# A graph network with attention and experts on one core: layer 2's joint products ahead of its spreads, the gate's arithmetic behind layer 1's last task, attention rows normalised on ScalarE, layer ends reordered

## What is computed

```python
for W, a_s, a_d, bg, R, g, b in layers:      # widths 3 -> 64 -> 128 -> 64
    h = _gat(x, src, dst, W, a_s, a_d, bg)   # softmax over a joint's edges, weighted sum of x @ W
    x = gelu(layer_norm(h + x @ R, g, b))
pose = layer_norm(x.reshape(n, J * 64) @ fpW + fpb, fng, fnb)
h = concatenate([pose, txt], axis=1)
h = h + attn(layernorm(h))     # silu, short convolution, normalised queries through a two-layer memory
h = h + ffn(layernorm(h))      # 8 experts of width 512, top two by router, gelu
```

## Time and profile before

| | us |
|---|---|
| median of 3 runs | 4580.26 (4574.3 to 4583.47) |
| the profiled execution | 4576.98 |
| its span, first to last instruction | 4575.1 |
| PE busy | 3889.9 (85%) |
| DVE busy | 3668.4 (80%) |
| ACT busy | 2318.4 (51%) |
| POOL busy | 1527.8 (33%) |

### The profile page before, as it was taken

The page is one execution under the profiler, slowest core; times in us unless marked ns, Lnnn a source line. Parts: engine busy times, 40 slices in busy tenths (PEclk is TensorE's granted clock), DMA queues, the critical chain, the costliest instruction groups (busy, mean ns, idle before and its releaser), DMA issues.

```text
span 4575.1 us, 62001 instructions
## 1 busy us (share of the span) xinstructions
PE 3889.9 (85%) x22762; PEld 1797.7 (39%) x22762; DVE 3668.4 (80%) x6623; ACT 2318.4 (51%) x3705; POOL 1527.8 (33%) x1513
## 2 busy tenths in 40 slices
PE   4878898888988888898888988888888888988888
PEld 2232343434334343343334434343343433434345
DVE  3878888788887888878788887888878888887872
ACT  2544455454545545455454555545455454554543
POOL 2524324252432524324252332524315243242410
PEclk8898999999999999999999999999999999999999
DMA  2000000000000000000000000000000000000000
GB/s 91 1 3 1 2 5 1 3 3 3 3 1 3 3 3 3 2 5 1 3 3 3 4 1 3 3 3 3 1 6 1 3 3 2 5 1 3 3 2 6
DMA packets 22815, 22.95 MB, mean 5 GB/s; under 512 B 3378, under 2 KB 21818, under 8 KB 22122
## 3 DMA queue, kind: packets, MB, share of 16 engines
q1 hardware_dynamic: 22506, 18.93, 1.4%
HBM read 14.72 MB, written 4.19 MB: 4 GB/s over the span
## 4 chain that ended last, share of the span: by engine, by line
DVE 48%; PE 34%; issue 9%; ACT 8%; POOL 1%; DVEq 0%; SPq 0%; DMA 0%; ACTq 0%; POOLq 0%
DVE R L2068 13%; PE bank L1033 6%; PE bank L1042 5%; DVE X L2073 4%; PE bank L764 3%; PE bank L836 3%; DVE X L1767 2%; PE bank L902 2%; DVE R L2043 2%; ACT X L1403 2%; DVE X L2105 2%; PE bank L776 2%; DVE Ho L2254 2%; DVE R L2046 1%; PE bank L680 1%
## 5 line engine op out<-in xcount | busy, mean ns | idle before, releaser
L576 POOL TENSOR_TENSOR X<-X,R 128x512 f32<-128x512 f32 (+1 forms) x624 | 801.0, 1284 | 1134.0 <-DVE X L2073 1131.3
L2068 DVE TENSOR_TENSOR R<-bank,R 128x1024 f32<-128x1024 f32 (+1 forms) x624 | 738.4, 1183 | 47.9 <-DVE X L2073 1.0
L2105 DVE TENSOR_TENSOR X<-X,bank 128x1024 f32<-128x1024 f32 (+2 forms) x432 | 484.7, 1139 | 248.4 <-PE bank L804 124.9
L1033 PE MATMUL bank<-XT,c_w 128*128 128x512 f32 x1024 | 565.6, 670 | 90.4 <-DVE R L2068 49.9
L1403 ACT ACTIVATE X<-X,c_vec 128x1024 f32<-128x1024 f32 (+2 forms) x432 | 498.1, 1173 | 217.8 <-DVE X L2105 214.4
L1042 PEld LDWEIGHTS bank<-c_w,SQ 128*128 128x128 f32 x4096 | 492.1, 192 | 95.8 <-issue 89.0
L1042 PE MATMUL bank<-c_w,SQ 128*128 128x128 f32 x4096 | 514.5, 278 | 0.0
L940 PE MATMUL bank<-X,WR 64*128 64x512 f32 (+1 forms) x832 | 482.1, 661 | 36.4 <-DVE Ho L2254 31.4
L1444 ACT ACTIVATE R<-bank 128x512 f32<-128x512 f32 (+1 forms) x416 | 241.2, 580 | 527.0 <-PE bank L902 296.6
L902 PE MATMUL bank<-R,c_W 64*128 64x512 f32 (+1 forms) x832 | 473.9, 651 | 37.6 <-ACT R L1446 24.1
L2073 DVE SCALAR_TENSOR_TENSOR X<-bank,bgc,R 128x512 f32<-128x512 f32 (+1 forms) x624 | 456.0, 731 | 31.7 <-PE bank L956 10.0
(11 more groups left out here) (287 smaller groups left out, 6675.9 us busy)
## 6 DMA issues: line engine op xcount, KB each, us to landing
c_w<-in_w SPq DMA_DIRECT2D x2, 2048.0 KB
out<-Ho SPq DMA_DIRECT2D x32, 128.0 KB, 1.9
c_fpW<-in_fpW SPq DMA_DIRECT2D x1, 3200.0 KB
X<-in_x SPq DMA_DIRECT2D x34, 75.0 KB, 2.0
X<-in_txt SPq DMA_DIRECT2D x32, 64.0 KB, 1.9
X<-in_sel SPq DMA_DIRECT2D x1, 600.0 KB
X<-in_sel SPq DMA_DIRECT2D x1, 300.0 KB
X<-in_raw SPq DMA_DIRECT2D x1, 256.0 KB
```

The costliest lines, as they stand in the source:

```text
L576: TT(dst, dst, TQ[:, k % 3, 0:cols], ALU.subtract).then_inc(zs_ok, 1)
L1033: mm(hidden_bank(e, m), w1[:, k * P:k * P + P], XT2[:], start=True, stop=True).then_inc(hid_ps, 1)
L2068: TT(TQ[:, k % 3:4:3 - k % 3, 0:cols], bR[k % 2][:, :, 0:cols], both, ALU.mult).then_inc(t_ok, 1)
L2105: TT(dst, dst, b, ALU.mult).then_inc(u_ok, 1)
```

## The change

- **Layer 2.** From n = 1 on PE issues `product_d` of the next task ahead of `spread_alpha`. DVE does `joint_differences` of the next task between its multiplication 2068 and its sum 2073, no longer after the sum.
- **The gate.** The six parts of `top_two` stand behind the last task of layer 1, ahead of `rstd`.
- **The attention's norm** moves from DVE (four instructions, subtract and multiply in one) to ACT (eight: four with the mean as bias and scale -1, four with the standard deviation's inverse as scale), after its copies of n = 1 and n = 2. The sign is taken back in `token_columns` (scale -1). In the window `add_expert` 7 now stands ahead of the moments.
- **Layer ends with experts.** `up` unit 0 writes bank 0 and waits for ACT's last copy (`d_sb`) instead of the last multiplication; that wait now stands ahead of unit 1. `HD` uses slots 2 to 5, and ACT does `hidden` unit 0 of experts 0 and 4 ahead of its last square, as soon as the last but one `variance` is done. Before the sums are turned, PE waits for that `hidden`.
- **POOL's `mean_differences`** waits for the third exp (`exp_ok`), no longer for the copied scores.

```diff
-        HD = SQ[:, 0:MT, :]
+        HD = SQ[:, 2:2 + MT, :]
+            if e in (0, 4):
+                return bank[(0, 2, 1, 2)[m]]
...
             def mean_differences(s, l):
-                pool.wait_ge(s_ok, s * 2 + l)
+                pool.wait_ge(exp_ok, s * 7 + 3 * l + 1)
...
@@ TensorE, graph_layer
+                    early = l == 2 and n > 0
+                    if early and n + 1 < NT[l]:
+                        product_d(s, l, n + 1)
                     spread_alpha(s, l, n)
-                    if n + 1 < NT[l]:
+                    if not early and n + 1 < NT[l]:
                         product_d(s, l, n + 1)
...
                 if tail:
-                    pe.wait_ge(t_ok, s * AGG + T0[l] - NT0 + NT[l] + 1)
+                    pe.wait_ge(d_sb, s * AGG + T0[l] - NT0 + NT[l])
                     up(s - 1, e, (0,))
                 variance(s, l, BATCHES[l] - 2)
                 if tail:
+                    pe.wait_ge(t_ok, s * AGG + T0[l] - NT0 + NT[l] + 1)
                     up(s - 1, e, (1,))
                 variance(s, l, BATCHES[l] - 1)
+                if tail:
+                    pe.wait_ge(hid_sb, (s - 1) * E * MT + e * MT + 2)
...
@@ ScalarE, graph_layer
+                    if l == 1 and n in (1, 2) and tail:
+                        attention_norm(s - 1, n - 1)
+                    if n == NT[l] + 2 and moe:
+                        hidden(s - 1, 0 if l == 1 else 4, (0,))
                     if n >= 3:
                         square(s, l, n - 3)
...
+            def attention_norm(t, part):
+                act.wait_ge(an_ok, t + 1)
+                if part == 1:
+                    act.wait_ge(hc_ok, t + 1)
+                for k in range(4):
+                    if part == 0:
+                        last = A_(Xn[:, k, :], HN[:, k, :], ACT.Identity, bias=mv[:, k, 0:1], scale=-1.0)
+                    else:
+                        last = A_(Xn[:, k, :], Xn[:, k, :], ACT.Copy, scale=rs[:, k:k + 1])
+                last.then_inc(ho_ok if part else hc_ok, 1)
...
@@ hidden on ScalarE
+                if units == (0,) and e in (0, 4):
+                    act.wait_ge(v_ps, (t + 1) * NBATCH + B0[2 if e else 1] + BATCHES[2 if e else 1] - 1)
...
@@ VectorE, neighbours
                 if l == 2:
-                    joint_differences(s, n)
+                    if n == 0:
+                        joint_differences(s, 0)
...
                 TT(TQ[:, k % 3:4:3 - k % 3, 0:cols], bR[k % 2][:, :, 0:cols], both, ALU.mult).then_inc(t_ok, 1)
+                if l == 2 and n + 1 < NT[l]:
+                    joint_differences(s, n + 1)
...
@@ VectorE, window and iteration
                 if tail:
                     attention_out(t)
-                    attention_moments(t)
                 if moe and main:
                     add_expert(t - 1, 7)
                 if tail:
-                    inverse_std(4)
+                    attention_moments(t)
+                    inverse_std(4, an_ok)
...
-                    if moe and n == 2:
-                        attention_norm(t)
                     if moe and n == 7:
                         logits(t)
-                    if moe and 12 <= n <= 22 and n % 2 == 0:
-                        top_two(t, (n - 12) // 2)
+                if moe:
+                    for part in range(6):
+                        top_two(t, part)
```

More of the change, by code:

```diff
@@ L391, in build @@
         ho_ok = sem("ho_ok")
+        an_ok = sem("an_ok")
+        hc_ok = sem("hc_ok")
         lg_ps = sem("lg_ps")
@@ L1598, in iteration @@
                 if moe:
-                    hidden(t, 0)
+                    hidden(t, 0, (1, 2, 3))
                 rstd_out(s, 1)
@@ L1621, in iteration @@
                 if moe:
-                    hidden(t, 4)
+                    hidden(t, 4, (1, 2, 3))
                 rstd_out(s, 2)
@@ L2198, in attention_moments @@
                 moments([HN[:, k, :] for k in range(4)])
-            def attention_norm(t):
-                for k in range(4):
-                    last = TS(Xn[:, k, :], HN[:, k, :], mv[:, k, 0:1], rs[:, k:k + 1], ALU.subtract, ALU.mult)
-                last.then_inc(ho_ok, 1)
             def logits(t):
```

17 lines of the change are left out of this document (9 added, 8 removed).

## The result

| | before | after |
|---|---|---|
| median of the runs, us | 4577.28 (4571.99 to 4583.47) | 4306.11 (4305.8 to 4307.07) |
| span of the profiled execution, us | 4575.1 | 4304.0 |
| mean granted clock of TensorE | 0.950 | 0.974 |
| DVE busy, us | 3668.4 | 3451.0 (80%) |
| PE busy, us | 3889.9 | 3816.6 (89%) |

The ratio of the times is 0.9407, with a 95% interval of 0.9391 to 0.9424. The prediction was 4310 us in a range of 4275 to 4375.

The account below looks back on a forecast made before the run. DVE was taken to bound both graph loops, PE the layer ends. Terms 30 + 91 + 43 + 70 + 32 + 5 - 1 = 270 us took the profiled 4577 to 4307, predicted as 4310 us, range 4275 to 4375.

Parts of the forecast that it names:

- part 1: Layer 1's loop: moving the attention's norm from DVE to ACT saves 2.03 us in each of 15 steps, 30 us.
- part 2: Layer 1's loop: taking out the gate's six parts saves 6.04 us in each of 15 steps, 91 us.
- Part 3: Layer 1's end: the gate fills DVE's idle time, the wait falls from 7.1 to 4.2 us; 43 us, low end 17.
- Part 4: Layer 2's loop: POOL's stops of DVE's differences go, 6.4 less 2.0 us added, 4.4 in 16 steps, 70 us.
- Part 5: Ahead of the layers: edge sums no longer meet POOL's work, 1.3 us in layer 2 and 0.7 in layer 1; 32 us.
- Part 6: Layer 2's end: DVE's next-step coordinates fill it; 0.3 us a step, 5 us gained, with 0 and 15 as bounds.
- this rival: Layer ends: the clock stays at 1.2 GHz, part 3 gives 17 and part 6 nothing, 4341; chance 0.20 shared with PE bounding layer 1.
- the bound in layer 1: Rival, layer 1's loop: PE sets the time at 2.25 us a task, losing 36 us, 4346; chance 0.20 shared with the clock at the ends.
- the "slower" rival: Layer 1's loop at the lower clock, 3.4 us a task, 30 us a step, 450 us in all: 4760; chance 0.04.

Follow-up runs that it names:

- run 5: The changed kernel with both layer ends as before; gate, norm, layer 2's loop and GpSimd's wait stay changed: 4302.7 us.
- run 3: The changed kernel with the gate's six parts back between tasks 12 to 22 of layer 1: 4420.52 us.
- run 6: The changed kernel with up unit 0 waiting for the last multiplication again, not ScalarE's last copy, at both layer ends: 4318.33 us.
- run 1: The changed kernel with layer 2's loop as before, joint_differences behind the sum and product_d behind spread_alpha: 4369.44 us.
- run 9: The changed kernel with two extra passes of up unit 0's product in TensorE's gap at layer 2's end: 4288.85 us.
- run 10: The changed kernel with layer 2's end reordered: one extra pass of up unit 0, unit 1 ahead of the last but one variance, last square ahead of hidden: 4268.05 us.
- run 11: The changed kernel with TQ's four slots as two pairs, so a multiplication no longer waits for the sum ahead of it: 4268.22 us.
- run 7: The changed kernel with the attention's norm on VectorE again, four instructions behind the third task of layer 1: 4350.47 us.
- run 2: The changed kernel with product_d behind spread_alpha again in all of layer 2, VectorE's order staying changed: 4316.46 us.

## Why the prediction was right, and where it wasn't

**Parts 1 and 2 (norm and gate in the loop): right.** The loop lost 8.13 us against 8.07. The count of DVE's instructions was enough, since PE kept up and ACT's 0.32 us for each of the norm's eight instructions held nobody. What I left out is that a pause of DVE also stops PE, whose clock can then fall. Undoing part 1 cost 44 us, not 30 (some 5 of it perhaps by chance), and undoing part 2 cost 114, not 91.

**Part 3 (end of layer 1): right in size, wrong in cause.** The step that failed is "I take 2.9, since the gap that came ahead of the low clock is filled". With the gap open, if only by 0.65 us (run 5), the clock is at 1.00 all the same, and the end is 5.14; with the gate back in the loop (run 3) it is 0.68 although the gap is filled, and the end is 6.8. Whether a gap of 1.4 to 1.7 us, as before, would have been enough by itself no run shows. So of the 44.8 us of this stage some 7 belong to the new order at the end (runs 5 and 6 give 0.47 and 0.71 us a step), and the rest to the gate's departure from the loop: its work fits into the wait, and its pauses no longer bring the clock down. The count from the last sum was off as well. Counted from the sum's end (2246.97), as the 4.2 and the 7.1 are, I had the variance of tasks 20 to 23 and unit 1 done at 1.2, the last variance at 1.85 and the chain at 3.3. They are done at 2.0 (2248.98), 2.7 (2249.71) and 4.15 (2251.12). The 0.8 us is there from the first of these: that variance starts 0.12 us ahead of the sum's end and takes 2.1 with unit 1. It did no harm because the gate takes as long, by chance to 0.03 us.

The Trainium skill (TensorE: Matmul & The Clock Gate, Part 1) ties the lower clock to TensorE idling. The runs agree, but the idle time that counted was the 1.9 us in the loop, ahead of the place where I looked for it.

**Part 4 (layer 2's loop): right in mechanism, 0.4 us a step too large.** The stops went, all of them, and run 1 brought exactly them back. The term that was off is "the wait of 0.30 us for product 2 stays". Since DVE now asks for it ahead of the first sum and not behind, it waits 0.68 us. That is 0.38 x 16 = 6 us, the difference of 70 and 64.

**Part 5 (edge sums): low by 12.** The two stages gained 44 us and not 32, and undoing this part cost 48. The layer 2 share was 21 as predicted. In the window I had capped the gain at 0.7 us a step by ACT's exps (the 1.16 in that sum is the 1.14 of the earlier trace rows); the stage lost 1.5. From the first edge sum to the reciprocal it is 10.66 us before (2290.10 to 2300.76) and 9.77 after (2164.97 to 2174.74), so 0.9. The other 0.6 lies behind, from `add_expert` 6 to the loop: 6.46 us before (2312.72 to 2319.18) and 5.83 after (2186.70 to 2192.53). There an instruction of the moments took 0.63 us (2315.85) and takes 0.17 now (2190.81). I had costed the moved `add_expert` 7 at nothing; that it is this move which saves the 0.46 is read from the rows and was not tested by itself.

**Part 6 (end of layer 2): wrong.** I gave it a gain of 5 us; it cost 7. The step that failed is "the steps with an idle of 0.5 us keep it": in the ends at the higher clock that idle time is 0.87 now, and the end 5.56 instead of 5.20. In run 5, with the old order at the end, the only such end takes 5.32. So some 0.12 us comes with the new loop, behind which the last square but one starts 0.51 us after the last sum's start and not 0.39. The other 0.24 comes with the new order at the end, where the last square stands behind `hidden` (0.69 us). The second step that failed is that the others "may win up to 2.7, if PE stays at the higher clock". It didn't stay: eleven ends run partly at the lower clock, not five.

It looks as if drawing `up` unit 0 forward had opened the gap, since it was 1.52 us in the kernel before:

```profile
2216.59 1.12 PE L1033 MATMUL bank<-XT,c_w 128*128 128x512 f32 x2 [1.52 <-DVE R L2068]
```

The runs say otherwise. With the new loop the gap is 2.49 us in the old order (run 5) and 2.62 in the new; with the old loop it is 3.04 in the new order (run 1), and 3.04 in the old wherever the clock was up until then (four steps of the kernel before; the last has 4.13). The 1.52 stands in the ten steps in which the clock had fallen earlier, inside layer 2's loop: in the step above the stretch 2210.3 to 2213.6 has a granted clock of 0.50, behind an idle time of PE of 2.18. There it cost nothing, as DVE sets the time of that loop. In the new loop that idle time is 0.89, the clock stays up, and falls at the end instead. Why it stayed up in the old loop of run 1 too, in all steps with experts, is open. Run 9 shows that PE's idle time at the end is what the lower clock hangs on, and run 10 that the stage can be made 28 us shorter, by three edits at once.

Some of the errors cancel: 12 us more in part 5, 3 in the loop of layer 1 and 2 at its end, against 6 less in part 4 and 12 less in part 6.

**The rivals.** PE was not the bound in layer 1, but by 0.04 us a task instead of the 0.07 of the prediction (run 11). The clock did stay low at one layer's end, but at layer 2's, for which this rival had priced 5 us, and not at layer 1's, for which it had 26. A loop at the lower clock did come, for nine us, in step 0, where there is neither norm nor gate. DVE's first sum of step 0, and the stretch around it:

```profile
129.49 0.75 DVE L2106 SCALAR_TENSOR_TENSOR X<-bank,bgc,R 128x512 f32<-128x512 f32 x1 [3.78 <-PE bank L960]
```

```profile
124.00:134.00 10.00, 10.00 (x25) 2.72 (x26) 4.43 (x7) 2.57 (x6) 2.82 (x3) 0.51 0.00 0
```

PE is busy all of the time there and too slow by half: that loop took 58.90 us against 55.48 before. This is the mechanism of the "slower" rival. It isn't an effect that the change always has: in this step the loop took 55.5 us in runs 5, 7, 9, 10 and 2, and 58.4 to 58.9 in the others that start from the changed kernel.

## What to carry to other kernels

Cost a pause on the bounding engine twice: once for itself, and once for what the engine next to it does while it has nothing to do. Here a quarter of the gate's price (31 of 114 us, run 3) was paid after the gate was over. When you shorten or fill one idle stretch, look at the others near it: the clock may fall behind another one, and that costs only where PE's work is what the rest waits for. And when a forecast comes out right, undo its parts one by one before you teach its reasons: the total of this one was within 4 us, with one part's cause wrong and another's sign.

## What the runs showed of the hardware

- Two instructions with two SBUF inputs each, one on DVE and one on POOL, take 1.65 and 1.27 us when they start together and 0.55 and 1.28 apart; 0.03 us between the one's end and the other's start is enough for no loss.
- TensorE's granted clock in a stretch depended on what came ahead of it: pauses of 1.2 and 1.9 us in the loop left 0.68 in a stretch where PE was busy for 5.91 of 6.70 us (run 3). Behind gaps of 2.62 us at layer 2's end the clock fell in eleven of fifteen steps, and two passes of a useless product in each of these gaps were worth 17 us (run 9).
- Where the clock falls is partly chance: ends of the same code came as 5.56 and as 7.10 us in one execution, and the work before the first loop took 122 to 130 us in kernels that don't differ there (runs 10 and 9). Differences of under some 8 us between single profiles should not be read as effects of an edit.
